# Attention score stage: order of items, pairing of score products and values on TensorE

## The chip, the cores and the metric

One Trainium2 chip, one core. The metric is the device time of one execution in microseconds, lower is better; the median of several executions counts.

## The reference, cut to what matters

The model has two layers of mixed blocks; the change touches only the first layer's attention (x is 2 batches x 512 tokens x 256 features, 16 query heads of 16 features on 4 key heads, causal):

```
q, k, v = x @ Wq.T + bq, x @ Wk.T + bk, x @ Wv.T + bv      # 16, 4, 4 heads of 16
q, k = _rope(q, N_EMBD), _rope(k, N_EMBD)
k, v = repeat(k, 4), repeat(v, 4)
att = einsum('bhqd,bhkd->bhqk', q, k) / sqrt(16)
att = softmax(where(causal, att, -inf))
y = einsum('bhqt,bhtd->bhqd', att, v)
return y @ Wo.T + bo
```

Around it stand layer norms, two mixture-of-experts blocks before and after, and a second layer with a gated delta rule. Their code is not changed.

## The kernel before, in words

`attention` (L816) has three blocks of instructions, each closed by a barrier of all engines. The first makes the layer norm and the projections. The second is the score stage. The third is the output projection. Each engine runs its own list in order and waits on semaphores.

In the score stage each key head ("group" g, 0 to 3) owns 32 of the 128 partitions (`SLOT`): 16 features, then one row for the running maximum. A "pair" is one of 8 combinations of batch b and r (the query head within its group), so four heads, one per group, are worked on together. 512 tokens are four tiles of 128 (`HT`). A pair has 8 items: a group half `gp` (groups 0 and 1, or 2 and 3) and a tile. `item(n)` (L810) gives them: the half changes every four items, the tile with each item. There are 64 items.

Each item has three products on TensorE:

- `rows_of_scores` (L968): queries of tile t against keys 0 to t, width (t + 1) x 128, two groups, 32 partitions each; then two bf16 matmuls of 128 x 128 (L976) that add the causal mask on the diagonal tile. VectorE takes the negative maximum of each row (`maximum`, L1071).
- `keys_of_scores` (L979): keys of tile j against queries j to 3, width 512 - 128 j, two groups. ScalarE takes the exponential into pT (L1050), GpSimd clears what lies under the diagonal (L1063).
- `values` (L990): v, 128 keys x 32 columns per group, against pT, the same width. The result of group g goes to 32 partitions of one PSUM bank, added over the key tiles.

An fp32 product shows as two records in the trace. The maxima of a pair must be known before its `keys_of_scores`: `turn_max` (L1001) transposes them and VectorE adds them to q (`take_max`, L1074). So `rows` runs `AHEAD` = 10 items before `keys`. `values` runs `LAG` = 2 items behind it. When a pair is complete ScalarE copies y (`copy_y`, L1039), TensorE transposes it (`turn_y`, L1011) and VectorE divides (`normalise`, L1080).

Score results go to three slots of two PSUM banks each, in rotation. In the steady state the order of places is `keys(n)`, `rows(n + AHEAD)`, `keys(n + 1)` and so on. `slot_free` (L964) makes each wait for the reader of the place three earlier: `keys(n)` waits for the maximum of the `rows` issued two items before, `rows` waits for the exponential of item n - 1. pT has `PT_BUFS` = 4 buffers; an exponential waits for the values that read its buffer.

TensorE's list for one item is: `keys(n)`, `rows(n + AHEAD)`, perhaps a turn, `values(n - LAG)`. With AHEAD = 10 and the old order, `keys` and `rows` of one item stand in the same group half for tiles 0 and 1 and in opposite halves for tiles 2 and 3, and their widths are 512 and 384, 384 and 512, 256 and 128, 128 and 256.

Of the kernel before, what the change touches and what calls it, by code (L numbers as in the profile page):

```python
# [14 lines left out]
P = 128  # L15
BANK = 512
B, T, D = 2, 512, 256
# [3 lines left out]
HT = BANK // P  # L21
# [4 lines left out]
REP = HQ // HKV  # L26
SLOT = 32
# [774 lines left out]

HEADS = REP * B
ITEMS = HEADS * 2 * HT
AHEAD = 10
LAG = 2
PT_BUFS = 4


def item(n):  # L810

    pair, gp, j = n // (2 * HT), n // HT % 2, n % HT
    return pair, pair // REP, pair % REP, gp, j


def attention(nc, m, tag, WqT, bq, WkT, bk, WvT, bv, WoT, bo, table, rope_in):  # L816

    with ExitStack() as ctx:
# [4 lines left out]
        v = sb("v", [P, NT, HKV, SLOT])  # L823
# [109 lines left out]
        with ExitStack() as ctx2:  # L933
# [3 lines left out]
            pT = [sb2(f"pT{s}", [P, 2, T]) for s in range(PT_BUFS)]  # L937
# [6 lines left out]
            y_b, aux = ps[:, 6], ps[:, 7]  # L944
            aux_tiles = aux.rearrange("p (t g s) -> p t g s", t=HT, g=HKV)


            rows_place = lambda n: n if n < AHEAD else 2 * n - AHEAD + 1
            keys_place = lambda n: AHEAD + n + min(n, ITEMS - AHEAD)
# [12 lines left out]
            @block.tensor  # L962
            def _(pe):
                def slot_free(place):  # L964
                    if place >= 3:
                        pe.wait_ge(*used_by(place - 3))

                def rows_of_scores(n):  # L968
                    pair, b, r, gp, t = item(n)
                    slot_free(rows_place(n))  # L970
                    for i in range(2):
                        rows = slice((2 * gp + i) * SLOT, (2 * gp + i + 1) * SLOT)
                        pe.matmul(slot(rows_place(n))[:, i, 0:(t + 1) * P], qT[rows, r, b * T + t * P:b * T + (t + 1) * P],
                                  kT[rows, b * T:b * T + (t + 1) * P], start=True, stop=False)
                    for i in range(2):
                        mm = pe.matmul(slot(rows_place(n))[:, i, t * P:(t + 1) * P], ident[:], mask[:], start=False, stop=True)  # L976
                    mm.then_inc(s_ready, 1)

                def keys_of_scores(n):  # L979
                    pair, b, r, gp, j = item(n)  # L980
                    slot_free(keys_place(n))
                    if n % (2 * HT) == 0:
                        pe.wait_ge(q_ready, pair + 1)
                    for i in range(2):
                        rows = slice((2 * gp + i) * SLOT, (2 * gp + i + 1) * SLOT)
                        mm = pe.matmul(slot(keys_place(n))[:, i, 0:T - j * P], kT[rows, b * T + j * P:b * T + (j + 1) * P],
                                       qT[rows, r, b * T + j * P:(b + 1) * T], start=True, stop=True)
                    mm.then_inc(sT_ready, 1)

                def values(n):  # L990
                    pair, b, r, gp, j = item(n)
                    pe.wait_ge(p_ready, n + 1)
                    if n % (2 * HT) == 0 and pair:
                        pe.wait_ge(y_copied, pair)
                    for i in range(2):
                        g = 2 * gp + i
                        mm = pe.matmul(y_b[g * SLOT:(g + 1) * SLOT, j * P:T], v[:, b * HT + j, g, :], pT[n % PT_BUFS][:, i, 0:T - j * P],
                                       start=(j == 0), stop=(j == HT - 1))
                    mm.then_inc(pv_ready, 1)

                def turn_max(pair):  # L1001
                    pe.wait_ge(max_ready, 2 * HT * (pair + 1))
                    if pair >= 1:
                        pe.wait_ge(q_ready, pair)
                    if pair >= 2:
                        pe.wait_ge(y_done, pair - 1)
                    for t in range(HT):
                        mm = pe.transpose(aux[:, t * P:(t + 1) * P], neg_max[pair % 2][:, t].rearrange("p g s -> p (g s)"), m.ident[:])
                    mm.then_inc(turned, 1)

                def turn_y(pair):  # L1011
                    pe.wait_ge(y_copied, pair + 1)
                    pe.wait_ge(q_ready, min(pair + 2, HEADS))
                    if pair:
                        pe.wait_ge(y_done, pair)
                    for t in range(HT):
                        mm = pe.transpose(aux[:, t * P:(t + 1) * P], y_sb[pair % 2][:, t * P:(t + 1) * P], m.ident[:])
                    mm.then_inc(y_turned, 1)

                for n in range(AHEAD):  # L1020
                    rows_of_scores(n)
                turn_max(0)
                for n in range(ITEMS + LAG):
                    pair, step = n // (2 * HT), n % (2 * HT)
                    if n < ITEMS:
                        keys_of_scores(n)
                    if n + AHEAD < ITEMS:
                        rows_of_scores(n + AHEAD)
                    if step == 3 and pair:
                        turn_y(pair - 1)  # L1030
                    if step == 6 and pair + 1 < HEADS:
                        turn_max(pair + 1)
                    if n >= LAG:
                        values(n - LAG)
                turn_y(HEADS - 1)

            @block.scalar
            def _(act):
                def copy_y(pair):  # L1039
                    act.wait_ge(pv_ready, 2 * HT * (pair + 1))  # L1040
                    if pair >= 2:
                        act.wait_ge(y_turned, pair - 1)
                    nc.scalar.activation(y_sb[pair % 2][:], y_b, ACT.Copy).then_inc(y_copied, 1)

                for n in range(ITEMS):
                    j = n % HT
                    act.wait_ge(sT_ready, n + 1)
                    if n >= PT_BUFS:
                        act.wait_ge(pv_ready, n + 1 - PT_BUFS)
                    nc.scalar.activation(pT[n % PT_BUFS][:, :, 0:T - j * P], slot(keys_place(n))[:, :, 0:T - j * P],  # L1050
                                         ACT.Exp).then_inc(e_ready, 1)
                    if n % (2 * HT) == LAG - 1 and n > LAG:
                        copy_y(n // (2 * HT) - 1)
                copy_y(HEADS - 1)

# [10 lines left out]
            @block.vector  # L1066
            def _(dve):
                def maximum(n):
                    pair, b, r, gp, t = item(n)
                    dve.wait_ge(s_ready, n + 1)  # L1070
                    nc.vector.tensor_reduce(neg_max[pair % 2][:, t, 2 * gp:2 * gp + 2, HD], slot(rows_place(n))[:, :, 0:(t + 1) * P],  # L1071
                                            AX_X, ALU.max, negate=True).then_inc(max_ready, 1)

                def take_max(pair):  # L1074
                    pair, b, r, gp, t = item(pair * 2 * HT)
                    dve.wait_ge(turned, pair + 1)
                    q = qT[:, r, b * T:(b + 1) * T]
                    nc.vector.tensor_tensor(q, q, aux, ALU.add).then_inc(q_ready, 1)

                def normalise(pair):  # L1080
                    pair, b, r, gp, t = item(pair * 2 * HT)
                    dve.wait_ge(y_turned, pair + 1)
                    nc.vector.reciprocal(rden[pair % 2][:], aux_tiles[:, :, :, HD]).then_inc(rden_ready, 1)
                    dve.wait_ge(rden_ready, pair + 1)
                    y = m.xn[:, b * HT:(b + 1) * HT, :].rearrange("p t (g r d) -> p t g r d", g=HKV, r=REP)[:, :, :, r, :]
                    nc.vector.tensor_tensor(y, aux_tiles[:, :, :, 0:HD], rden[pair % 2][:, :, :, None].broadcast_to([P, HT, HKV, HD]),
                                            ALU.mult).then_inc(y_done, 1)

                dve.wait_ge(zeroed, 2)
                for n in range(AHEAD):  # L1090
                    maximum(n)
                take_max(0)
                for n in range(ITEMS):
                    pair, step = n // (2 * HT), n % (2 * HT)
                    if n + AHEAD < ITEMS:
                        maximum(n + AHEAD)
                    if step == 3 and pair:
                        normalise(pair - 1)
                    if step == 6 and pair + 1 < HEADS:
                        take_max(pair + 1)  # L1100
                normalise(HEADS - 1)

        with ExitStack() as ctx2:
# [1027 lines left out]
```

## Time and profile before

| what | value |
| --- | --- |
| median of 3 runs | 2441.1 us (2438.06 to 2441.97) |
| profiled execution, time | 2445.81 us |
| profiled execution, span | 2444.1 us |
| TensorE busy | 2069.8 us (85%) |
| VectorE busy | 1286.1 us (53%) |
| ScalarE busy | 999.1 us (41%) |
| GpSimd busy | 391.8 us (16%) |
| mean granted TensorE clock | 0.921 |

The span is the time that the profiler saw of one execution. Busy time is the union of an engine's instructions; register, branch and semaphore instructions are not counted. PE is the matmul side of TensorE, PEld its weight loads, which can lie beside matmuls. The granted clock is the share of the full TensorE clock (1.00 is 2.4 GHz, 0.50 is 1.2 GHz). The second block of the attention lies between 156 and 316 us.

### The profile page before, as it was taken

The numbers are of one execution on the slowest core, as the hardware profiler recorded it, in microseconds if no ns is written. First come the engines' busy times: TensorE is split into PE (matmuls) and PEld (weight loads), VectorE is DVE, ScalarE is ACT, GpSimd is POOL, SyncE is SP. The second block draws the span as 40 slices with busy tenths as digits, with TensorE's granted clock in tenths as the row PEclk, the third lists the DMA queues.
The fourth block names the chain that finished last, engine by engine and source line by source line (L and its number), as shares of the span: only waits on it lengthen the run. The fifth ranks groups of instructions, "written<-read, shape, count | busy, mean of one in ns | idle before, by whom it ended". The sixth has DMA issues, their size and how long they took to land. (4 is left out here: it accounts for less than half of the span.)

```text
span 2444.1 us, 52330 instructions
## 1 busy us (share of the span) xinstructions
PE 2069.8 (85%) x20606; PEld 1507.8 (62%) x20606; DVE 1286.1 (53%) x2928; ACT 999.1 (41%) x2476; POOL 391.8 (16%) x442
## 2 busy tenths in 40 slices
PE   7889989598824698999999999999999998958884
PEld 4543355487722467677767766776677666737774
DVE  4434444412225466776677667766776775531222
ACT  2113321222202355646664655565556654512221
POOL 0001100110020022122212222122122211202002
PEclk9969989699956699999999999999999998958997
DMA  1100001721011110111011101110111010045001
GB/s 45 34 11 1 1 14 39 278 76 27 16 44 42 22 31 14 34 26 31 19 35 24 32 19 36 23 32 19 36 24 32 19 28 10 11 137 205 30 20 61
DMA packets 148345, 100.08 MB, mean 41 GB/s; under 512 B 88640, under 2 KB 134992, under 8 KB 148112
## 3 DMA queue, kind: packets, MB, share of 16 engines
q1 hardware_dynamic: 144368, 86.59, 12.5%
q0 software_dynamic: 3744, 10.23, 1.5%
q8 instruction: 165, 2.70, 0.5%
q14 instruction: 68, 0.56, 0.1%
HBM read 83.28 MB, written 13.50 MB: 40 GB/s over the span
## 5 line engine op out<-in xcount | busy, mean ns | idle before, releaser
L1582 PE MATMUL dn_ps<-xnT,dn_w 128*128 128x512 f32 x512 | 260.3, 634 | 33.6 <-DMA dn_w<-in_W_qkvz_dram 22.1
L1935 DVE SCALAR_TENSOR_TENSOR dn_cv<-dn_raw,dn_cw,dn_cv 128x1024 f32<-128x1024 f32 x192 | 270.6, 1409 | 1.2
L588 PE MATMUL g_ps<-g_w,xnT 128*128 (+1 forms) x736 | 166.1, 379 | 0.0
L1582 PEld LDWEIGHTS dn_ps<-xnT,dn_w 128*128 128x128 f32 x512 | 91.5, 198 | 114.9 <-issue 100.2
L577 PE MATMUL g_ps<-g_xT,g_w_now 128*128 128x128 f32 x960 | 117.5, 282 | 50.3 <-DVE g_w_now L716 50.3
L1727 PE MATMUL dn_ps<-dn_wout,dn_oT 128*128 128x256 f32 x512 | 150.0, 418 | 6.2 <-ACT dn_oT L1742 3.7
L1742 ACT ACTIVATE dn_kdk<-dn_ps,dn_cf 128x128 f32<-128x128 f32 x256 | 80.0, 364 | 180.4 <-PE dn_ps L1622 180.4
L516 ACT ACTIVATE xnT<-g_ps,g_b_now 128x128 f32<-128x128 f32 x240 | 68.4, 368 | 206.3 <-PE g_ps L577 206.3
L577 PEld LDWEIGHTS g_ps<-g_xT,g_w_now 128*128 128x128 f32 x960 | 112.6, 196 | 61.5 <-issue 61.5
L588 PEld LDWEIGHTS g_ps<-g_w,xnT 128*128 128x128 f32 x736 | 136.4, 190 | 16.7
L1742 ACT ACTIVATE dn_raw<-dn_ps 128x512 f32<-128x512 f32 x128 | 76.4, 598 | 147.1 <-PE dn_ps L1582 147.1
L1589 PE MATMUL dn_ps<-dn_w,xnT 128*64 128x128 f32 x2048 | 125.8, 276 | 0.0
L1891 POOL TENSOR_TENSOR xn<-xn,dn_zt 128x256 f32<-128x256 f32 x64 | 49.9, 780 | 428.8 <-DVE xn L2047 377.0
L1589 PEld LDWEIGHTS dn_ps<-dn_w,xnT 128*64 128x64 f32 x2048 | 111.2, 137 | 9.3 <-issue 7.2
L1891 POOL TENSOR_TENSOR dn_o<-dn_o,dn_zt 128x256 f32<-128x256 f32 x64 | 50.0, 781 | 415.5 <-DVE dn_o L2047 364.8
L1742 ACT ACTIVATE dn_vp<-dn_ps,dn_cf 128x128 f32<-128x128 f32 x256 | 79.4, 361 | 90.5 <-PE dn_ps L1690 90.5
L485 POOL DMA_INDIRECT g_xs<-xn_rows,g_token_u x46 | 44.2, 961 | 436.5 <-DVE g_token_u L684 223.4
L2068 DVE TENSOR_TENSOR x_res<-x_res,dn_ps 128x256 f32<-128x256 f32 x128 | 53.7, 420 | 106.5 <-PE dn_ps L1727 106.5
L1727 PEld LDWEIGHTS dn_ps<-dn_wout,dn_oT 128*128 128x128 f32 x512 | 91.3, 199 | 27.8 <-issue 8.2
L705 DVE COPY g_xT<-g_ps 128x256 f32<-128x256 f32 x46 | 19.5, 425 | 167.1 <-PE g_ps L558 167.1
L1742 ACT ACTIVATE dn_qs<-dn_ps,dn_cf 128x128 f32<-128x128 f32 x224 | 70.4, 369 | 76.6 <-PE dn_ps L1677 76.0
L1885 POOL TENSOR_TENSOR dn_kept<-dn_state,dn_cf 128x512 f32<-128x512 f32 x96 | 100.9, 1051 | 0.0
(309 smaller groups left out, 4375.8 us busy)
## 6 DMA issues: line engine op xcount, KB each, us to landing
g_w<-in_fc_dram SPq DMA_DIRECT2D x32, 1024.0 KB, 13.0
dn_w<-in_W_qkvz_dram SPq DMA_DIRECT2D x16, 768.0 KB, 4.5
dn_x<-dn_cum_rows SPq DMA_DIRECT2D x32, 256.0 KB, 3.9
ys_rows<-g_ys SPq DMA_DIRECT2D x46, 128.0 KB, 1.7
dn_wout<-in_W_out_dram SPq DMA_DIRECT2D x16, 256.0 KB, 2.8
f_gate<-in_gateT_dram SPq DMA_DIRECT2D x16, 128.0 KB, 2.2
f_up<-in_upT_dram SPq DMA_DIRECT2D x16, 128.0 KB, 2.3
f_down<-in_downT_dram SPq DMA_DIRECT2D x16, 128.0 KB, 2.4
```

The source lines that it names most:

```text
L485: nc.gpsimd.indirect_dma_start(xs[:, i % RING, :], None, xn_rows, bass.IndirectOffsetOnAxis(ap=token_u[:, i:i + 1], axis=0)).then_inc(xs_l ...
L516: last = nc.scalar.activation(hT[i % 2][:, f, :], h_b[2 * (i % 2) + half][:, q * P:(q + 1) * P], ACT.Gelu, bias=bias[:, f:f + 1])
L577: last = pe.matmul(h_b[2 * (i % 2) + half][:, q * P:(q + 1) * P], of(k, f), xT[i % 2][:, k, :], start=(k == 0), stop=(k == KD - 1))
L588: last = pe.matmul(y_b[i % 2][:, 0:D], hT[i % 2][:, f, :], of(f), start=(f == 0), stop=(f == NF - 1))
L1582: mm = pe.matmul(to, w[:, k, W_COL[u] * P:(W_COL[u] + 1) * P], m.xnT[:, k, b * T:(b + 1) * T], start=(k == 0), stop=(k == KD - 1))
L1589: mm = pe.matmul(to[half(h), part(n)], m.xnT[:, k, b * T + c * C:b * T + (c + 1) * C], w[:, k, W_COL[4 + h] * P:(W_COL[4 + h] + 1) * P], s ...
L1727: mm = pe.matmul(projected, tokens, wout[:, h, :], start=(h == 0), stop=(h == GRP - 1))
L1742: copy = lambda out, in_, **kw: nc.scalar.activation(out, in_, ACT.Copy, **kw)
L1885: nc.gpsimd.tensor_tensor(kept[:], state[:], last_decay.broadcast_to([P, B, GRP, DK]), ALU.mult).then_inc(s_["kept_r"], 1)
L1891: nc.gpsimd.tensor_tensor(o[f][:, c], o[f][:, c], zt[f][:, c], ALU.mult).then_inc(s_["oz_r"], 1)
L1935: ins = nc.vector.scalar_tensor_tensor(out=cv[:, u], in0=raw[:, u, :, tap:tap + T], scalar=cw[:, g, tap:tap + 1], in1=cv[:, u], op0=ALU.mu ...
L2068: nc.vector.tensor_tensor(xs, xs, projected, ALU.add).then_inc(s_["y_done"], 1)
```

## The change

A pair's items are now ordered key tile first: the tile changes every two items, the group half with each. `rows_item` gives `rows(n + 12)` the width of `keys(n)` and the opposite group half. `values` is called once for two items, for all four groups. `turn_max` moves from step 6 to step 5, `turn_y` from step 3 to step 7, the copy of y to the exponential of item 2 of a pair. AHEAD is 12, LAG 4, PT_BUFS 6. Work per product is unchanged.

```diff
--- before.py
+++ after.py
@@ -802,15 +802,21 @@
 
 HEADS = REP * B
 ITEMS = HEADS * 2 * HT
-AHEAD = 10
-LAG = 2
-PT_BUFS = 4
-
-
-def item(n):
-
-    pair, gp, j = n // (2 * HT), n // HT % 2, n % HT
+AHEAD = 12
+LAG = 4
+PT_BUFS = 6
+
+
+def keys_item(n):
+
+    pair, j, gp = n // (2 * HT), n // 2 % HT, n % 2
     return pair, pair // REP, pair % REP, gp, j
+
+
+def rows_item(n):
+
+    pair, t, gp = n // (2 * HT), (AHEAD // 2 - 1 - n // 2) % HT, 1 - n % 2
+    return pair, pair // REP, pair % REP, gp, t
 
 
 def attention(nc, m, tag, WqT, bq, WkT, bk, WvT, bv, WoT, bo, table, rope_in):
@@ -966,7 +972,7 @@
                         pe.wait_ge(*used_by(place - 3))
 
                 def rows_of_scores(n):
-                    pair, b, r, gp, t = item(n)
+                    pair, b, r, gp, t = rows_item(n)
                     slot_free(rows_place(n))
                     for i in range(2):
                         rows = slice((2 * gp + i) * SLOT, (2 * gp + i + 1) * SLOT)
@@ -977,7 +983,7 @@
                     mm.then_inc(s_ready, 1)
 
                 def keys_of_scores(n):
-                    pair, b, r, gp, j = item(n)
+                    pair, b, r, gp, j = keys_item(n)
                     slot_free(keys_place(n))
                     if n % (2 * HT) == 0:
                         pe.wait_ge(q_ready, pair + 1)
@@ -987,30 +993,31 @@
                                        qT[rows, r, b * T + j * P:(b + 1) * T], start=True, stop=True)
                     mm.then_inc(sT_ready, 1)
 
-                def values(n):
-                    pair, b, r, gp, j = item(n)
-                    pe.wait_ge(p_ready, n + 1)
-                    if n % (2 * HT) == 0 and pair:
+                def values(first):
+                    pair, b, r, _, j = keys_item(first)
+                    pe.wait_ge(p_ready, first + 2)
+                    if first % (2 * HT) == 0 and pair:
                         pe.wait_ge(y_copied, pair)
-                    for i in range(2):
-                        g = 2 * gp + i
-                        mm = pe.matmul(y_b[g * SLOT:(g + 1) * SLOT, j * P:T], v[:, b * HT + j, g, :], pT[n % PT_BUFS][:, i, 0:T - j * P],
-                                       start=(j == 0), stop=(j == HT - 1))
-                    mm.then_inc(pv_ready, 1)
+                    for gp in range(2):
+                        for i in range(2):
+                            g = 2 * gp + i
+                            mm = pe.matmul(y_b[g * SLOT:(g + 1) * SLOT, j * P:T], v[:, b * HT + j, g, :],
+                                           pT[(first + gp) % PT_BUFS][:, i, 0:T - j * P], start=(j == 0), stop=(j == HT - 1))
+                    mm.then_inc(pv_ready, 2)
 
                 def turn_max(pair):
                     pe.wait_ge(max_ready, 2 * HT * (pair + 1))
                     if pair >= 1:
                         pe.wait_ge(q_ready, pair)
-                    if pair >= 2:
-                        pe.wait_ge(y_done, pair - 1)
+                    if pair >= 3:
+                        pe.wait_ge(y_done, pair - 2)
                     for t in range(HT):
                         mm = pe.transpose(aux[:, t * P:(t + 1) * P], neg_max[pair % 2][:, t].rearrange("p g s -> p (g s)"), m.ident[:])
                     mm.then_inc(turned, 1)
 
                 def turn_y(pair):
                     pe.wait_ge(y_copied, pair + 1)
-                    pe.wait_ge(q_ready, min(pair + 2, HEADS))
+                    pe.wait_ge(q_ready, min(pair + 3, HEADS))
                     if pair:
                         pe.wait_ge(y_done, pair)
                     for t in range(HT):
@@ -1026,12 +1033,12 @@
                         keys_of_scores(n)
                     if n + AHEAD < ITEMS:
                         rows_of_scores(n + AHEAD)
-                    if step == 3 and pair:
+                    if n % 2 == 0 and n >= LAG:
+                        values(n - LAG)
+                    if step == 5 and pair + 1 < HEADS:
+                        turn_max(pair + 1)
+                    if step == 7 and 1 <= pair < HEADS:
                         turn_y(pair - 1)
-                    if step == 6 and pair + 1 < HEADS:
-                        turn_max(pair + 1)
-                    if n >= LAG:
-                        values(n - LAG)
                 turn_y(HEADS - 1)
 
             @block.scalar
@@ -1043,13 +1050,13 @@
                     nc.scalar.activation(y_sb[pair % 2][:], y_b, ACT.Copy).then_inc(y_copied, 1)
 
                 for n in range(ITEMS):
-                    j = n % HT
+                    j = n // 2 % HT
                     act.wait_ge(sT_ready, n + 1)
                     if n >= PT_BUFS:
-                        act.wait_ge(pv_ready, n + 1 - PT_BUFS)
+                        act.wait_ge(pv_ready, 2 * ((n + 2 - PT_BUFS) // 2))
                     nc.scalar.activation(pT[n % PT_BUFS][:, :, 0:T - j * P], slot(keys_place(n))[:, :, 0:T - j * P],
                                          ACT.Exp).then_inc(e_ready, 1)
-                    if n % (2 * HT) == LAG - 1 and n > LAG:
+                    if n % (2 * HT) == LAG - 2 and n > LAG:
                         copy_y(n // (2 * HT) - 1)
                 copy_y(HEADS - 1)
 
@@ -1066,19 +1073,19 @@
             @block.vector
             def _(dve):
                 def maximum(n):
-                    pair, b, r, gp, t = item(n)
+                    pair, b, r, gp, t = rows_item(n)
                     dve.wait_ge(s_ready, n + 1)
                     nc.vector.tensor_reduce(neg_max[pair % 2][:, t, 2 * gp:2 * gp + 2, HD], slot(rows_place(n))[:, :, 0:(t + 1) * P],
                                             AX_X, ALU.max, negate=True).then_inc(max_ready, 1)
 
                 def take_max(pair):
-                    pair, b, r, gp, t = item(pair * 2 * HT)
+                    _, b, r, _, _ = keys_item(pair * 2 * HT)
                     dve.wait_ge(turned, pair + 1)
                     q = qT[:, r, b * T:(b + 1) * T]
                     nc.vector.tensor_tensor(q, q, aux, ALU.add).then_inc(q_ready, 1)
 
                 def normalise(pair):
-                    pair, b, r, gp, t = item(pair * 2 * HT)
+                    _, b, r, _, _ = keys_item(pair * 2 * HT)
                     dve.wait_ge(y_turned, pair + 1)
                     nc.vector.reciprocal(rden[pair % 2][:], aux_tiles[:, :, :, HD]).then_inc(rden_ready, 1)
                     dve.wait_ge(rden_ready, pair + 1)
@@ -1094,10 +1101,10 @@
                     pair, step = n // (2 * HT), n % (2 * HT)
                     if n + AHEAD < ITEMS:
                         maximum(n + AHEAD)
-                    if step == 3 and pair:
+                    if step == 5 and pair + 1 < HEADS:
+                        take_max(pair + 1)
+                    if step == 7 and pair:
                         normalise(pair - 1)
-                    if step == 6 and pair + 1 < HEADS:
-                        take_max(pair + 1)
                 normalise(HEADS - 1)
 
         with ExitStack() as ctx2:
```

## Rows read from the trace of the kernel before

**Rows 1.** Stretches of the whole span: window, length, busy us of each engine, granted clock, DMA.
```profile
156.00:316.40 160.40, 156.40 (x960) 60.45 (x960) 62.64 (x88) 50.75 (x73) 26.97 (x66) 0.91 0.00 1
```

**Rows 2.** The same view, one period in the middle of the score stage.
```profile
195.63:213.27 17.64, 17.51 (x122) 6.85 (x120) 7.81 (x12) 6.23 (x9) 3.26 (x8) 1.00 0.00 1
```

**Rows 3.** Timeline, four items: start us, length us, engine, line, operation, shape, count.
```profile
213.38 1.13 PE L986 MATMUL at_ps<-at_qT,at_kT 32*128 32x512 f32 x4
...
214.34 0.81 PE L973 MATMUL at_ps<-at_kT,at_qT 32*128 32x384 f32 x4
...
214.56 1.02 ACT L1050 ACTIVATE at_pT<-at_ps 128x1024 f32<-128x1024 f32 x1 [1.88 <-PE at_ps L986]
...
215.09 0.28 PE L976 MATMUL at_ps<-at_mask,at_ident 128*128 128x128 bf16 x2
...
215.30 0.63 PE L997 MATMUL at_ps<-at_pT,at_v 128*32 128x256 f32 x4
...
215.86 0.91 PE L986 MATMUL at_ps<-at_qT,at_kT 32*128 32x384 f32 x4
...
216.61 1.02 PE L973 MATMUL at_ps<-at_kT,at_qT 32*128 32x512 f32 x4
...
216.82 0.81 ACT L1050 ACTIVATE at_pT<-at_ps 128x768 f32<-128x768 f32 x1 [1.24 <-PE at_ps L986]
...
217.56 0.29 PE L976 MATMUL at_ps<-at_mask,at_ident 128*128 128x128 bf16 x2
...
218.12 0.48 PE L986 MATMUL at_ps<-at_qT,at_kT 32*128 32x256 f32 x2
...
218.13 0.49 PE L973 MATMUL at_ps<-at_kT,at_qT 32*128 32x128 f32 x4
...
218.44 0.38 PE L986 MATMUL at_ps<-at_qT,at_kT 32*128 32x256 f32 x2
...
218.75 0.28 PE L976 MATMUL at_ps<-at_mask,at_ident 128*128 128x128 bf16 x2
...
218.98 1.05 PE L997 MATMUL at_ps<-at_pT,at_v 128*32 128x512 f32 x4
...
219.96 0.38 PE L986 MATMUL at_ps<-at_qT,at_kT 32*128 32x128 f32 x2
...
219.98 0.48 PE L973 MATMUL at_ps<-at_kT,at_qT 32*128 32x256 f32 x2
...
220.61 0.29 PE L976 MATMUL at_ps<-at_mask,at_ident 128*128 128x128 bf16 x2
...
220.73 0.61 PE L1017 MATMUL at_ps<-ident,at_y_sb 128*128 128x128 f32 x4
...
222.04 0.70 PE L986 MATMUL at_ps<-at_qT,at_kT 32*128 32x512 f32 x2
```

**Rows 4.** Timeline around the turn of the maxima.
```profile
209.77 0.28 PE L976 MATMUL at_ps<-at_mask,at_ident 128*128 128x128 bf16 x2
...
210.18 0.66 PE L1008 MATMUL at_ps<-ident,at_neg_max 128*128 128x128 f32 x4
...
210.77 1.05 PE L997 MATMUL at_ps<-at_pT,at_v 128*32 128x512 f32 x4
```

**Rows 5.** Stretches at the lower clock, and where it rises.
```profile
158.00:162.00 4.00, 4.00 (x14) 1.27 (x12) 1.65 (x2) 0.00 (x0) 0.00 (x0) 0.50 0.01 2
...
186.00:190.00 4.00, 4.00 (x24) 1.48 (x24) 1.61 (x2) 1.02 (x1) 0.47 (x2) 0.98 0.02 4
```

**Rows 6.** Timeline, TensorE before the first pair and at its first product.
```profile
169.47 0.80 PE L973 MATMUL at_ps<-at_kT,at_qT 32*128 32x128 f32 x4
...
170.52 1.22 PE L973 MATMUL at_ps<-at_kT,at_qT 32*128 32x256 f32 x4
...
173.80 2.08 PE L986 MATMUL at_ps<-at_qT,at_kT 32*128 32x512 f32 x4 [0.87 <-DVE at_qT L1078]
```

**Rows 7.** Timeline, the last operation of the score stage.
```profile
315.93 0.42 DVE L1086 TENSOR_TENSOR xn<-at_ps,at_rden 128x256 f32<-128x256 f32 x1
```

## Prediction

> **What bounds the kernel now.** I read the totals by stretch first, then the timeline of one period of the attention's score stage, then the same stage where it begins and ends. The stage runs from 156.0 to 316.4 us of the profiled execution, and in its 160.4 us TensorE is busy for 156.4; VectorE has 62.6, ScalarE 50.8 and GpSimd 27.0, and the DMA engines have nothing [rows 1]. So only TensorE's time counts here, and whatever lies outside this stage (2284 us of the span) is not touched. In the middle of the stage one head of one batch (a "pair", eight items) takes 17.64 us, with TensorE busy for 17.51, VectorE for 7.81 and ScalarE for 6.23 [rows 2].
>
> The timeline [rows 3] shows what TensorE does in the four items of one group half. The reader is to see three things. First, a score product is four records (two groups, and each fp32 product in two parts), and two groups stream at the same time: the 512 wide product lets the next one start after 214.34 - 213.38 = 0.96 us, and the two parts of one group, one behind the other, make up that time. Second, where `keys_of_scores` and `rows_of_scores` use different halves of the groups, all four groups stream together: at 218.12 and 218.13 both begin, `rows` (128 wide, four records) is through in 0.49 us, while the second parts of `keys` (256 wide) begin at 218.44, and the mask follows at 218.75. Third, this happens only for the two narrow items of four (218.12 and 219.96); the two wide items run `keys` and `rows` one after the other, because they use the same rows of the array.
>
> **What a product costs.** Let s be what one part of a product streams: 0.427, 0.320, 0.213 and 0.107 us for widths 512, 384, 256 and 128 (0.95 us from the 512 wide `rows` at 216.61 to its mask is 2 x 0.427 + 0.1; 0.75 from 214.34 to 215.09 is 2 x 0.32 + 0.1). A score block costs 2s + 0.2 when it stands behind other work: the four-group block of 256 and 128 took 0.63 = 0.427 + 0.2, and the one of 128 and 256 took 0.65 [rows 3]. Two masks cost 0.21 to 0.22 (215.09 to 215.30). Values cost 2s + 0.13: 0.98 for 512 (218.98 to 219.96), 0.56 for 256. The turn of the maxima costs 0.78 more than the 0.22 between mask and values elsewhere (209.77 to 210.77, [rows 4]), the turn of y 1.43 - 0.22 - 0.77 = 0.44 (220.61 to 222.04, [rows 3]).
>
> **Parts of the change, TensorE's work alone, for one pair.**
> - Score blocks side by side: the new order gives `keys` of item n and `rows` of item n + 12 the same width and opposite halves. Eight blocks, two of each width: 4 x 1.067 + 8 x 0.2 = 5.9 us (0.206 taken for 0.2). Before, from the first product to the mask, they are 1.71 (213.38 to 215.09), 1.70 (215.86 to 217.56), 0.63 and 0.65, twice each: 9.4 us. Saved: 3.5.
> - Values of two items in one call, in four groups of 32 columns: 4 x 0.13 + 2 x 1.067 = 2.65 us, before twice that, 5.3. Saved: 2.65. The trace shows two column groups together at full rate (512 wide: 0.98 us for four records that stream 0.427 each) but never four. Bounds: nothing lost, or the second pair of groups waits for the first, +2.13 us a pair. I take nothing lost, because the change from one to two groups, and from two row groups to four, cost nothing in the nearest rows, and I keep the other end as a rival.
> - Masks 8 x 0.215 = 1.7 and turns 1.2 us stay.
>
> Sum 5.9 + 2.65 + 1.7 + 1.2 = 11.5 us, against 17.6 (the same list for before: 9.4 + 5.3 + 1.7 + 1.2 = 17.6).
>
> **The wait that takes the place.** There are three score slots, used in the order keys, rows, keys. `rows` in item n needs the slot of `keys` of item n - 1, so it waits for that item's exponential. Today TensorE never waits for it in the steady state: 1 us of rows or values always lies between. With the blocks halved that cover is gone. Queued behind the waiting `rows` on TensorE are its masks, the values and all later items; VectorE's next maximum waits for it too. The exponentials take 1.02 and 0.81 us for the two widest items [rows 3] and less for the others, and begin 0.05 us after the product's last record ends (213.38 + 1.13 against 214.56), which is 0.16 behind the end of streaming. One pair walked through, times from its first product: block 512 at 0, masks 1.06, values (256) 1.29, `keys` 1.85, its `rows` only at 2.24, when the first exponential (1.17 to 2.19) is done; masks 3.30; `keys` 384 at 3.53, `rows` at 4.09 behind the second exponential; masks 4.93, values (128) 5.16, block 384 at 5.51, not delayed; masks 6.35; `keys` 256 at 6.58, `rows` at 7.32 behind the second exponential of width 384; masks 7.96, values (512) 8.19, block 256 at 9.17, turn 10.03, block 128 at 10.62, values (384) 11.27, block 128 at 12.04, turn of y 12.69, end 13.25. The three waits delay by 0.4, 0.55 and 0.75 = 1.7 us, and 11.5 + 1.7 = 13.2. VectorE's work per pair (7.8) and ScalarE's (6.2) stay below that, GpSimd's 3.3 too; `keys` waits for a maximum of two items earlier, which is always done in this walk. PT_BUFS, LAG and the copy of y set no wait in it: pT has six buffers for a distance of at most six, and the copy of y fits ahead of the last exponential of width 384. So a steady pair saves 17.65 - 13.25 = 4.4 us.
>
> **The ends of the stage.** The loop ahead of the first pair now makes 12 row products instead of 10, alone and at the lower clock: the trace has 1.05 us for one 128 wide item at that place (169.47 to 170.52) and some 1.4 for a 256 wide one [rows 6]: +2.4. They are the same products that go from the end, but there they would have stood beside `keys` for nothing. The first pair begins at the lower clock, as now. Walked through with the low clock until 186.2 us, where it rises in the trace [rows 5], it takes 15.6 us instead of 22.9 in the same walk of the old order (-7.3). Pair 1: 13.6 (-4.1). Pairs 2 to 5: -4.4 each, -17.6. Pair 6, half without rows: 11.6 against 17.3, -5.7. The last pair with its turn and division: 11.6 against 15.4, -3.8. Sum: 2.4 - 7.3 - 4.1 - 17.6 - 5.7 - 3.8 = -36 us. The walk with the old order gives 161.1 us for the stage, where [rows 1, 7] have 160.4, so its error is below 1 us there.
>
> **Forecast.** The profiled execution took 2445.8 us (span 2444.1), 4.7 above the median of the runs shown; 2445.8 - 36 = 2409.8, and on the median 2441.1 it is 2405. If the clock rises at 176 rather than 186, it gains another 2.6; if only at 200, it loses 5.3. If each hand-over between engines cost 0.15 instead of 0.05 us, a pair would take 13.8 and the stage 4.6 more: 2410. Later stages can shift by a few us, as their low-clock stretches fall elsewhere.
>
> **A rule against it.** In the trace a 128 wide `rows` part is through before the second parts of `keys`, issued ahead of it, have begun (218.13 + 0.49 against 218.44 + 0.38, [rows 3]), so each row group goes on by itself. The Trainium skill, "TensorE: Matmul & The Clock Gate", section "Part 3: Packing small matmuls", says that matmuls start and end strictly in program order. By that rule the first part of the next group would stand behind the second part of this one, and blocks could not overlap as reckoned; the trace disagrees.
>
> **Rivals.**
> A. Four column groups don't stream at once (they share a read of pT's 128 partitions): the values keep their old price, a pair takes 15.4, the stage ends 17 us later than forecast: 2422. For it: four are nowhere in the trace. Against: two together cost nothing.
> B. Four row groups slow each other when all are 512 or 384 wide: the score blocks run as two halves, a pair takes 15.8, 18.6 us later: 2424. For it: full width on all four isn't shown. Against: the 256 and 128 blocks show no stretching of either.
> C. Neither overlaps (A and B together): a pair takes 18.0 and the stage as long as now: 2441, no change.
> D. Slower: the clock. From 158 to 162 us TensorE was busy for all of 4.00 us and was still granted 0.50, and it stayed so until 186 [rows 5]; so being busy alone does not bring the high clock. If the new order, with waits between shorter blocks, stayed at 1.2 GHz in this stage, a pair would cost 8.5 + 2.5 (blocks) + 2.9 (masks) + 4.9 (values) + 2.5 (turns) = 21.3 us and the stage 182 instead of 160.4: 2462. It decides as soon as more than about five of the eight pairs run at 1.2 GHz. Against: from 186 on the old order never fell back [rows 1, 2], and the new one uses more of the array in each microsecond.
>
> **Chances.** Forecast 0.70, with the dearer hand-overs (2410) 0.08 more, A 0.09, B 0.05, C 0.04, D 0.04. The range 2398 to 2425 holds the first four. About 0.2% (5 us) is what a measurement tells from no change: faster 0.92, same 0.04, slower 0.04.
>
> **What would show it.** In the profile after: a period of 13.2 us per pair with TensorE's `rows` of the wide items waiting for the exponential, three times in eight items; values of four groups starting within 0.02 us and the 512 wide ones over in 0.98 us; the block of two 512 wide products reaching its mask in 1.06 us; a stage of 124 to 125 us. A period of 15.4 with values of 1.8 us is A, with score blocks of 2 us B; a granted clock near 0.5 after 190 us is D. The forecast is wrong if the stage saves less than 28 us, or if the rest moves by more than 6.

## The result

The changed kernel takes 2403.5 us (median of 4 runs, 2403.1 to 2409.0) against 2441.05, a ratio of 0.9844 (95% interval 0.9823 to 0.9865). The forecast was 2405, from 2398 to 2425. Five more runs beside the experiments gave 0.9846 (0.9829 to 0.9863). Its profiled execution took 2403.5 us, with a span of 2401.8.

The view of stretches, changed kernel, shows the score stage and what comes behind it. Its first line answers to [rows 1], with the same columns.

```profile
154.50:280.90 126.40, 123.15 (x960) 52.00 (x960) 62.72 (x88) 50.59 (x73) 27.02 (x66) 0.87 0.01 1
280.90:2401.80 2120.90, 1778.22 (x19254) 1365.92 (x19254) 1155.48 (x2646) 924.31 (x2361) 358.76 (x353) 0.93 0.16 45
```

The stage has the same 960 matmuls and takes 126.4 instead of 160.4 us: 34.0 less. The other 8.3 us of the profiled pair's difference lie outside (1.5 ahead of the stage, 6.8 behind it), where no instruction was changed. In the 50 us behind the stage the granted clock was 0.76 before and 0.86 after:

```profile
316.40:366.40 50.00, 39.63 (x139) 26.91 (x140) 26.43 (x89) 12.16 (x24) 0.00 (x0) 0.76 0.06 17
```

```profile
280.90:330.90 50.00, 38.37 (x148) 25.22 (x149) 26.90 (x90) 12.65 (x25) 0.00 (x0) 0.86 0.10 25
```

The first is the kernel before, the second the changed one. Such stretches fall differently in each execution; the runs of one kernel on one chip spread by 3 to 25 us (by 74 in same_half, below).

The timeline of the changed kernel, TensorE and ScalarE in the first five items of a steady pair, answers to [rows 3]. L992 is `keys_of_scores`, L979 `rows_of_scores`, L982 the masks, L1004 `values`, L1057 the exponential.

```profile
218.30 0.70 PE L992 MATMUL at_ps<-at_qT,at_kT 32*128 32x512 f32 x2
...
218.31 0.70 PE L979 MATMUL at_ps<-at_kT,at_qT 32*128 32x512 f32 x2
...
219.37 0.29 PE L982 MATMUL at_ps<-at_mask,at_ident 128*128 128x128 bf16 x2
219.47 1.02 ACT L1057 ACTIVATE at_pT<-at_ps 128x1024 f32<-128x1024 f32 x1 [1.35 <-PE at_ps L992]
...
219.59 0.64 PE L1004 MATMUL at_ps<-at_pT,at_v 128*32 128x256 f32 x8
...
220.16 0.70 PE L992 MATMUL at_ps<-at_qT,at_kT 32*128 32x512 f32 x2
...
220.55 0.70 PE L979 MATMUL at_ps<-at_kT,at_qT 32*128 32x512 f32 x2
...
221.83 0.91 PE L992 MATMUL at_ps<-at_qT,at_kT 32*128 32x384 f32 x4
...
222.41 0.30 PEld L979 LDWEIGHTS at_ps<-at_kT,at_qT 32*128 32x128 f32 x4 [0.28 <-ACT at_pT L1057]
...
224.90 0.70 PE L992 MATMUL at_ps<-at_qT,at_kT 32*128 32x256 f32 x4
...
225.65 0.30 PEld L979 LDWEIGHTS at_ps<-at_kT,at_qT 32*128 32x128 f32 x4 [0.45 <-ACT at_pT L1057]
...
226.50 1.06 PE L1004 MATMUL at_ps<-at_pT,at_v 128*32 128x512 f32 x8
...
227.50 0.48 PE L992 MATMUL at_ps<-at_qT,at_kT 32*128 32x256 f32 x2
...
231.41 0.70 PE L992 MATMUL at_ps<-at_qT,at_kT 32*128 32x512 f32 x2
```

The reader sees: both 512 wide products begin together and the mask follows 1.07 us later (218.30 to 219.37; forecast 1.06). The values of four groups, 512 wide, are over in 1.00 us (226.50 to 227.50; 0.98). `rows` starts 0.39, 0.58 and 0.75 us behind `keys` in items 1, 2 and 4, twice with the exponential named as the releaser; the forecast had 0.39, 0.56 and 0.74. The period is 231.41 - 218.30 = 13.11 us (13.25), before 17.64.

### The profile page after: what moved, and what is told of

Its sections match the earlier page's. It is cut to its first block and busy times, and to the rows that moved or that the text cites. A ratio compares the mean times of both kernels' runs of the same rounds, so it can differ in the third digit from the quotient of the medians.

```text
span 2401.8 us, 52328 instructions
## 1 busy us (share of the span) xinstructions
PE 2025.8 (84%) x20606; PEld 1490.4 (62%) x20606; DVE 1286.1 (54%) x2928; ACT 1000.3 (42%) x2476; POOL 391.6 (16%) x442
## 5 line engine op out<-in xcount | busy, mean ns | idle before, releaser
L723 DVE COPY g_ys<-g_ps 128x256 f32<-128x256 f32 x46 | 19.5, 424 | 154.7 <-PE g_ps L588 154.7
## 6 DMA issues: line engine op xcount, KB each, us to landing
g_w<-in_fc_dram SPq DMA_DIRECT2D x32, 1024.0 KB, 13.1
```

## The experiments

All score variants run the same number of products, but for the added ones of the three burst runs. Lengths of the stage and of a pair are from one profiled execution each. The runs fell on different chips, on which the kernel before takes 2441 to 2448 us; a ratio is always against the runs of the kernel before on the same chip.

**values_two_groups.** The values of two column groups at a time, all else as changed (the waits on the values and the step of the copy of y follow, not shown).

```diff
-                    pe.wait_ge(p_ready, first + 2)
-                    for gp in range(2): ...      # four groups
-                    if n % 2 == 0 and n >= LAG:
+                    pe.wait_ge(p_ready, n + 1)
+                    for i in range(2): ...       # the item's two groups
+                    if n >= LAG:
                         values(n - LAG)
```

> The changed kernel with one part undone: values are called per item again, for the two groups of its half; order, pairing of the score products, AHEAD, LAG and PT_BUFS stay. My theory (four column groups stream at the price of two, rows wait for exponentials): the values cost 4 x 0.13 + 2 x 1.07 = 2.65 us more per pair of TensorE's time, but they now lie between all items and cover most of the three waits (1.7 us), so a steady pair takes 15.0 instead of 13.1 us and the stage 143 instead of 126: about 2420. Rival (four column groups share a stream, nothing gained by them): the pair stays at 13.1 and the time at 2403.

```profile
156.20:300.10 143.90, 140.84 (x960) 55.12 (x960) 63.63 (x88) 50.87 (x73) 27.08 (x66) 0.88 0.00 1
225.30:240.30 15.00, 15.00 (x121) 5.97 (x120) 7.95 (x11) 6.23 (x9) 3.27 (x8) 1.00 0.00 1
```

The stretches show a stage of 143.9 and a pair of 15.0 us, as expected. The time is 2429.5 us, ratio 0.9926 (0.9912 to 0.9940), on a chip where the kernel before took 2448.2: 19 us saved, where the expected 2420 meant 21. The clock rose as late after the start of the stage as in the changed kernel (34 us). So about half the gain (17.5 of 34 us) is the values in four groups.

**before_ahead_12.** The kernel before with `AHEAD = 12`. Opposite halves, opposite widths.

> The kernel before with AHEAD 12 instead of 10 and nothing else: now keys(n) and rows(n + 12) always stand in opposite halves, but with opposite widths (512 with 128, 384 with 256 and so on). My theory (a block lasts as long as its wider product): streams of a pair are 2 x 2 x (0.427 + 0.32 + 0.32 + 0.427) = 6.0 instead of 4.3 us with equal widths, a pair takes 16.5 us against 17.6 before, the first products take 2.4 to 4 us longer, the stage 153 to 154: about 2434. Rival (opposite halves are all that counts, width doesn't): a pair near 15, 2425. Rival (equal halves cost nothing): 17.6 a pair and some 2 us more than before, 2443.

Its timeline shows the widest and the narrowest product side by side, TensorE only:

```profile
232.06 0.70 PE L986 MATMUL at_ps<-at_qT,at_kT 32*128 32x512 f32 x2
232.07 0.49 PE L973 MATMUL at_ps<-at_kT,at_qT 32*128 32x128 f32 x4
232.59 0.59 PE L986 MATMUL at_ps<-at_qT,at_kT 32*128 32x512 f32 x2
233.12 0.28 PE L976 MATMUL at_ps<-at_mask,at_ident 128*128 128x128 bf16 x2
```

```profile
152.50:310.90 158.40, 155.21 (x960) 57.49 (x960) 62.42 (x88) 50.63 (x73) 27.11 (x66) 0.86 0.00 1
232.10:248.50 16.40, 16.40 (x126) 6.29 (x124) 7.79 (x12) 6.19 (x9) 3.27 (x8) 1.00 0.00 1
```

A block of 512 and 128 takes 1.06 us to its mask, the same as the block of 512 and 512 in the changed kernel. The pair takes 16.4 us (16.5 expected). But the stage takes 158.4, 5 more than expected. The clock rose only at some 196.5 us (0.50 from 194 to 196 us, 1.00 from 198 on), 44 us after the start of the stage instead of 30; by the prediction's walk, where a rise 14 us later costs 5.3 us, that is about the difference. The time is 2442.8 us, ratio 0.9978 (0.9961 to 0.9994): 5 us saved, where the expected 2434 meant 7. Opposite halves alone bring a pair from 17.64 to 16.4 us; with equal widths as well, values still in two groups (values_two_groups), it is 15.0. That run also has the new order and deeper buffers, so the second step is not equal widths alone.

**short_exp.** The changed kernel, exponentials over 128 of up to 512 columns; the rest of the softmax is left out (pT is set to zero once, ahead of the first exponential, not shown).

```diff
-                    nc.scalar.activation(pT[..][:, :, 0:T - j * P], slot(..)[:, :, 0:T - j * P], ACT.Exp)
+                    nc.scalar.activation(pT[..][:, :, 0:P], slot(..)[:, :, 0:P], ACT.Exp)
```

> The changed kernel with each exponential only over the first 128 columns of both groups (0.38 us instead of up to 1.02); the rest of pT holds zeros, so that part of the softmax is left out. All waits stay in place. My theory (three of eight rows wait for an exponential, 1.7 us a pair): those waits go, what is left is some waiting of keys for maxima, a pair takes 12.2 instead of 13.1 us, the stage 118 to 119 instead of 126: about 2396. Rival (TensorE is bound by its own work and never waits): 13.1 a pair, 2403.

```profile
216.20:228.10 11.90, 11.90 (x121) 5.32 (x120) 7.74 (x12) 3.66 (x9) 3.19 (x9) 1.00 0.01 1
```

```profile
218.02 0.70 PE L992 MATMUL at_ps<-at_qT,at_kT 32*128 32x512 f32 x2
218.03 0.70 PE L979 MATMUL at_ps<-at_kT,at_qT 32*128 32x512 f32 x2
...
219.31 0.59 PE L992 MATMUL at_ps<-at_qT,at_kT 32*128 32x384 f32 x2
219.63 0.59 PE L979 MATMUL at_ps<-at_kT,at_qT 32*128 32x384 f32 x2
```

In item 1 both products now start together (218.02 and 218.03), where the changed kernel has 0.39 us between. In item 2 a wait of 0.32 us is left (219.31 to 219.63), even for the short exponential, and as much in item 4 (222.12 to 222.44). A pair takes 11.9 us (12.2 expected), so the length of the exponentials is worth 13.1 - 11.9 = 1.2 us of a pair. The stage takes 126.4 - 117.6 = 8.8 us less than in the changed kernel:

```profile
156.00:273.60 117.60, 115.07 (x960) 49.40 (x960) 62.73 (x88) 30.14 (x73) 32.18 (x72) 0.87 0.01 1
```

The time, 2403.8 us on the chip with 2448.2 before, is a ratio of 0.9822 (0.9808 to 0.9836) against the changed kernel's 0.9844: some 5 us, and the two intervals overlap. About 2396 was expected. What lies behind the stage took 2126.5 us in this profile and 2120.9 in the changed kernel's, 5.6 more, with no instruction changed there.

**same_half.** `rows_item` returns half `n % 2` instead of `1 - n % 2`.

> The changed kernel with the other part undone: rows(n + 12) uses the same group half as keys(n), same width, so the two can't stand side by side; values in four groups stay. My theory: a pair takes 15.8 us (blocks 4s + 0.2 instead of 2s + 0.2, no wait for exponentials any more), the stage 144 to 145, about 2421. Rival (the gain came from the order and the deeper buffers, not from the row groups): 13 to 14 us a pair, about 2405.

```profile
156.20:386.40 230.20, 227.76 (x960) 94.83 (x960) 63.84 (x88) 50.52 (x73) 26.85 (x66) 0.51 0.00 1
231.50:260.20 28.70, 28.70 (x123) 12.25 (x122) 7.98 (x11) 6.23 (x9) 3.25 (x8) 0.50 0.00 1
```

Neither case was right. Three of four executions took 2514 to 2521 us and one 2447, so no ratio is given, and the profiled one is of the long kind. It shows a pair of 28.7 us at a granted clock of 0.50, which is 1.2 GHz, from 156 to 381 us, with TensorE busy for all 28.70. The other executions have no trace, but the mean granted clock of the whole execution goes with the time: 0.882 to 0.886 in the three long ones, 0.914 in the short one, 0.920 to 0.923 in those of the kernel before on the same chip. In the profiled execution, with two row groups at a time in the score products, and masks, values and turns between, the clock rose only in the last pair. Why one execution of four escaped stays open. This is what rival D describes, in another kernel.

**same_half_burst.** The same, with a burst ahead of the first turn of maxima:

```diff
+                def burst():
+                    for _ in range(8):
+                        pe.matmul(y_b, m.ident[:], kT[:, 0:T], start=True, stop=True)
...
+                burst()
                 turn_max(0)
```

> The kernel same_half (rows in the same group half as keys), which ran its whole score stage at 1.2 GHz in three of four executions, with eight fp32 products of 128 x 128 against 128 x 512 added behind the first 12 row products, ahead of the first keys; their result is overwritten. Theory (the full array raises the clock; two row groups at a time are enough to hold it once it is up): 8 x 0.85 to 1.7 = 7 to 12 us for the added products, then pairs of 15.8 us at 2.4 GHz, 2425 to 2432. Rival (two row groups at a time cannot hold the clock): it falls back and most pairs take 28.7 us, 2500 to 2530.

```profile
174.84 9.72 PE L987 MATMUL at_ps<-at_kT,ident 128*128 128x512 f32 x16
```

```profile
176.60:185.90 9.30, 8.43 (x21) 3.66 (x19) 0.69 (x1) 0.00 (x0) 0.00 (x0) 0.81 0.00 0
215.60:231.20 15.60, 15.60 (x123) 7.47 (x122) 7.93 (x12) 6.23 (x9) 3.29 (x9) 1.00 0.00 1
```

The clock rose at some 180 us (0.73 from 178 to 182 us, 1.00 from there), 5 us into the burst, and stayed at 1.00 to the end of the stage. A pair takes 15.6 us (15.8 expected), the time is 2429.7 us (10 runs, 2419.8 to 2437.2), ratio 0.9934 (0.9911 to 0.9957). So with 9.7 us of added work it takes 88 us less than the median of same_half, and none of ten executions was of the long kind, against three of four. The two runs were on different chips (same_half had 2448.2 before, this one 2444.9), and same_half was not run on the second; that the burst and not the chip did it rests on the clock, which rose in the middle of the burst. It also prices the other half of the change: with the clock up, two row groups instead of four cost 15.6 - 13.1 = 2.5 us a pair. With the 15.0 - 13.1 = 1.9 us of values_two_groups that is 4.4 of the 4.5 us by which a pair became shorter, so little is left for the order, the buffers and the places of the turns; both halves were not undone in one run.

**burst_4_start, burst_8_start.** `prologue_pairs` (below) with 4 or 8 of those products as the first of the stage.

> prologue_pairs with four of those full-array products as the first thing that TensorE does in the score stage. Theory (low clock there because the array was idle or little used; a full-array product raises it, as in the projections, where it rose 4 us after they began): 5 us for the products, then the row products, VectorE's maxima as their next limit, at 2.4 GHz: stage 119 to 121 against 120.0 in prologue_pairs, 2398 to 2402. Rival (row products alone let the clock fall again): 5 to 6 us slower than prologue_pairs, 2407.

> The same with eight products. If four raise the clock, the other four only add 4 x 0.85 = 3.4 us: 2403 to 2405. If four don't and eight do: the first keys begin 9 to 10 us behind the start of the stage plus the row products at 2.4 GHz (12 us), the clock does not wait for the pairs, 2403. If neither: 2412.

```profile
154.00:158.00 4.00, 3.58 (x5) 1.70 (x6) 0.00 (x0) 1.28 (x1) 0.99 (x2) 0.57 0.03 6
158.00:167.80 9.80, 8.43 (x56) 3.69 (x54) 5.41 (x8) 0.00 (x0) 0.00 (x0) 1.00 0.00 1
167.80:188.30 20.50, 19.62 (x94) 8.46 (x95) 8.76 (x12) 4.73 (x6) 2.04 (x5) 0.50 0.00 1
188.30:279.80 91.50, 89.20 (x816) 38.48 (x814) 48.03 (x70) 44.58 (x67) 23.92 (x59) 1.00 0.00 1
```

These are the stretches with four. The clock rose at 157.6 us and fell again at 167.8, while TensorE worked through the first row products with gaps (busy 8.43 of 9.80 us, the rest waits for maxima), and came back only at 188.3. Time 2406.9 us, as the rival had it (2407), ratio 0.9841 (0.9809 to 0.9872), no better than prologue_pairs without it (0.9824). With eight it is 2415.0, 0.9884 (0.9843 to 0.9924): worse than all three cases that I had set down, with the same fall, 4 us later. In these two runs a burst does not pay, because the clock does not last through what follows.

**turn_y_at_3.** `turn_y(pair - 1)` and its division at step 3 instead of 7, with the waits that this order needs.

> The changed kernel with turn_y moved from step 7 to step 3 (and its division), where the next rows (item 4) wait 0.74 us for the exponential of item 3. My theory (that wait covers the turn): 0.25 to 0.44 us less per pair, 1 to 3 us in all, about 2401. Rival (the turn delays the keys of item 4 and so its exponential and all behind it): no change or 1 us more, 2403 to 2405.

```profile
211.85 0.60 PE L1024 MATMUL at_ps<-ident,at_y_sb 128*128 128x128 f32 x4
212.39 0.48 PE L992 MATMUL at_ps<-at_qT,at_kT 32*128 32x256 f32 x2
212.70 0.48 PE L979 MATMUL at_ps<-at_kT,at_qT 32*128 32x256 f32 x2
...
218.01 0.70 PE L992 MATMUL at_ps<-at_qT,at_kT 32*128 32x512 f32 x2
218.34 0.70 PE L979 MATMUL at_ps<-at_kT,at_qT 32*128 32x512 f32 x2
```

In the timeline item 4 now waits 0.31 instead of 0.75 us, but item 0, which had none, waits 0.33: the turn had covered that. A pair takes 13.0 us. The time is 2409.4 us (2401 expected, 2403 to 2405 by the rival), ratio 0.9850 (0.9832 to 0.9868), no gain beside 0.9846. In this profile the clock fell in the last pair, before the stage ended, which it did not in the changed kernel's:

```profile
274.10:284.60 10.50, 9.04 (x52) 2.95 (x52) 1.35 (x4) 2.45 (x5) 1.98 (x5) 0.50 0.00 0
```

**after_again, prologue_pairs, both.** The changed kernel again, then with the first 12 row products two by two, then that with turn_y_at_3.

```diff
-                for n in range(AHEAD):
-                    rows_of_scores(n)
+                for n in range(0, AHEAD, 2):
+                    for i in range(2):
+                        rows_of_scores(n + i, masked=False)
+                    for i in range(2):
+                        add_mask(n + i)
```

> The changed kernel once more, beside the next three on one chip, with more rounds: 2403 us, ratio 0.984 to 0.985. Its stage is 34 us shorter; the rest of the gain is from low-clock stretches that fall elsewhere, so with another start of those stretches the time can be 5 us higher (one of four runs so far was).

> The changed kernel with the first 12 row products taken two by two (both products, then both pairs of masks), so that four row groups stream at once there too. My theory: the first keys begin 3.5 us earlier; if the clock rises when it did (187.8 us), the stage is 2 us shorter, about 2401.5. If denser work makes the clock rise earlier, a further 3 to 6 us: 2396 to 2398. Rival (VectorE's maxima bound that part, 12 of them take 8.9 us of 18.5): less than 1 us.

> Both edits of the two runs ahead of this one together: the sum of their effects, 2399 if the clock rises as in the changed kernel, 2394 to 2396 if earlier.

```profile
154.30:274.40 120.10, 116.57 (x960) 51.21 (x960) 62.08 (x88) 50.54 (x73) 26.95 (x66) 0.90 0.01 1
154.30:170.90 16.60, 15.41 (x76) 8.23 (x77) 8.97 (x13) 1.28 (x1) 0.99 (x2) 0.50 0.01 2
```

These are the stretches of prologue_pairs: its first `keys` come 16.6 us after the start, against 20.4 in the changed kernel (154.5 to 174.94), as expected, and the stage takes 120.1. Its clock rose at some 178 us (0.55 from 176 to 178 us, 1.00 from there), 24 us after the start. after_again's stage took 122.9 in its profile, since its clock rose at 180.7 and not at 188.3 us, also 24 us after the start. So the earlier rise needs no paired products, and with the clock alike the two stages differ by 2.8 us:

```profile
156.60:279.50 122.90, 119.68 (x960) 51.37 (x960) 62.75 (x88) 50.55 (x73) 26.90 (x66) 0.90 0.01 1
```

On one chip, 2442.1 before: after_again 2406.3 (2399.4 to 2410.5), prologue_pairs 2402.0 (2398.7 to 2405.9), ratio 0.9824 (0.9807 to 0.9841), both 2409.8, ratio 0.9856 (0.9834 to 0.9878). The sum expected of both (2399) did not come, as the turn brings nothing. prologue_pairs is 4 us better than the changed kernel by the medians, but the intervals overlap; that it is faster is likely and not shown.

## Why the prediction was right

- *Score blocks of four groups at 2s + 0.2, no stretching at 512*: shown by the 1.07 us block, and by before_ahead_12, where the narrow product in the other half is free. With the score products back in one half (same_half_burst, at the high clock) a pair takes 15.6 us, where rival B's price was 15.8.
- *Values of four column groups at the price of two*: the open term of the sum, taken at its lower bound. 1.00 us in the timeline; undoing it alone costs 17.5 us of stage, where rival A's price was 17. The period is 15.0 and not rival A's 15.4, since the values now lie between all items and cover part of the waits.
- *Three waits for exponentials, 1.7 us a pair*: the three starts were 0.39, 0.58 and 0.75 us late, as walked through. Shortening the exponentials gave back 1.2, and left 0.32 us of the second wait and as much of the third. The period came out 0.14 below the walk (13.25): from the masks to the next product a turn took 0.66 us both times (228.14 to 228.80, 230.75 to 231.41), where the walk had some 0.8.
- *Start of the stage*: the first `keys` came 20.4 us after the start against 17.9 before, +2.5 where +2.4 was forecast.
- *First pair*: this term was too large. The lines below are the first `keys` of pairs 0 and 1 in the changed kernel and of pair 1 in the kernel before (pair 0 is in [rows 6], at 173.80). The pair took 191.77 - 174.94 = 16.8 us against 195.74 - 173.80 = 21.9: 5.1 saved, 7.3 forecast. The walk of the old order had this pair 1.0 too long (22.9), and that of the new one 1.2 too short (15.6). The clock rose at 188.3 us, 33.8 after the start of the stage (before 30.3), so the pair ran for 13.4 us at the lower clock, where the walk had some 10 (176.2 to 186.2). At the walk's price, 5.3 us for a rise 14 us later, these 3.4 us cost 1.3. In after_again the clock rose after 24 us.

```profile
174.94 1.22 PE L992 MATMUL at_ps<-at_qT,at_kT 32*128 32x512 f32 x2 [0.87 <-DVE at_qT L1085]
191.77 0.70 PE L992 MATMUL at_ps<-at_qT,at_kT 32*128 32x512 f32 x2
```

```profile
195.74 0.70 PE L986 MATMUL at_ps<-at_qT,at_kT 32*128 32x512 f32 x2
```

- *Sum*: 36 us for the stage, 34.0 measured in that profile, 37.5 in after_again (160.4 - 122.9). The medians moved by 37.6, so 3.6 us of the gain lie beyond the stage of that profile and were forecast only as scatter of a few us. That the time came within 2 us of 2405 is in part luck: the stage saved 2 us less than reckoned and the rest happened to give more than that back. Between the two profiled executions the rest even moved by 8.3 us, more than the 6 that the forecast had set as a sign of being wrong. 4.7 of these are the distance of the profiled execution before from its median; the sign was set too tight for single profiles.
- *Rival D* lies near: changing one line of this kernel (same_half) put the profiled stage at 1.2 GHz for 225 of its 230 us, and three of four executions took some 70 us longer than the fourth. None of the nine executions of the changed kernel did that. The forecast's argument against it, that the new order uses more of the array at a time, fits that result but is not shown by it.
- *The rule of strict program order*, which the prediction takes from the Trainium skill, "TensorE: Matmul & The Clock Gate", section "Part 3: Packing small matmuls", does not hold here. The prediction's own figures show less than it says: the narrow records end at 218.13 + 0.49 = 218.62, behind 218.44, where the second parts of the wide product begin (they end at 218.82). before_ahead_12 is clear: all four records of the 128 wide product have ended (232.07 + 0.49) before the second parts of the wide one, issued ahead of it, start (232.59).

## What to carry to other kernels

Products that use few rows or columns of the array pay in pairs: put beside each other those that use different row (or column) groups and have the same width, since a block lasts as long as its widest member (512 beside 128 took 1.06 us, 512 beside 512 took 1.07). A walk through one period with the durations of the timeline, calibrated on the old order, gave the new period within 0.15 us, waits included; the uncertain part was the clock. Before an edit by which fewer parts of the array work at a time, look for stretches where TensorE is busy throughout and still granted 0.50: there a small change can cost more than all that was gained (some 70 us in three of four executions of same_half, against 37.6 gained).

## What the runs showed of the hardware

- A fully busy TensorE need not get 2.4 GHz. In the profile of same_half, with score products on two row groups at a time, it stayed at 1.2 GHz for 225 us, busy for 28.70 of 28.70 us of a pair. In that of same_half_burst the same products ran at 2.4 GHz to the end of the stage, after the clock had risen within 9.7 us of full-array products. So one stream of work was seen at either level, by what stood ahead of it; each is one profile, on two chips.
- Row groups go on independently: in before_ahead_12 the four records of a 128 wide product take 0.49 us beside a 512 wide one, as they do beside a 256 wide one [rows 3], and the wide one reaches its mask in 1.06 us.
- Four column groups reading 128 partitions each stream as fast as two: their eight records take 1.06 us at width 512, and the four of two column groups 1.05 before [rows 3].
- Not tried: whether the score stage holds 2.4 GHz if its first 12 row products are made dense enough, without VectorE's maxima between them.
